# A recommendation tower's pairwise dot products: the second tile's gram of each pair made sample by sample in two banks, packed by one transpose

## The reference

```
e = stack([tbl_f[ids[:, f]] for f in range(32)], axis=1)      # 2048 x 32 x 128
z = einsum('bfd,bgd->bfg', e, e)[:, iu, ju]                   # upper triangle: 496
h = concatenate([z, dense_ctx], axis=1)                       # 512
h = maximum(h @ W_top1 + b_top1, 0);  h = maximum(h @ W_top2 + b_top2, 0)
y = h @ W_top3                                                # 2048 x 1
```

## Time and profile before

| | |
|---|---|
| median of 3 executions | 439.18 us (438.72 to 439.19) |
| the profiled execution | 440.8 us |
| its span, first to last instruction | 438.9 us |
| TensorE matmuls busy | 396.6 us, 90% |
| VectorE busy | 337.4 us, 77% |
| GpSimd busy | 307.6 us, 70% |
| ScalarE busy | 121.7 us, 28% |
| mean granted TensorE clock | 0.984 |

### The profile page before, as it was taken

How to read it: one execution, slowest core, us unless ns; L and a number is a source line. 1 busy time by engine, 2 the same in 40 slices (tenths; PEclk the granted TensorE clock), 3 DMA queues, 4 the chain that set the end, 5 groups by cost and what they waited for, 6 DMA issues and landing times.

```text
span 438.9 us, 11697 instructions
## 1 busy us (share of the span) xinstructions
PE 396.6 (90%) x4672; PEld 371.2 (85%) x4672; DVE 337.4 (77%) x873; ACT 121.7 (28%) x220; POOL 307.6 (70%) x324
## 2 busy tenths in 40 slices
PE   0469677999999999999999999999999999999967
PEld 0468577989999889989999989999999999998866
DVE  3789949999498958899498949899589949891510
ACT  1254410133213321233113321233214311332323
POOL 5777877777777777777777777777777777777100
PEclk9998998899999999999999999999999999999999
DMA  6999953435234332424332442436332543332000
GB/s 131 235 240 215 218 174 80 104 78 100 77 83 77 99 98 57 99 75 103 74 81 72 106 93 58 97 79 100 73 86 72 102 93 66 89 74 54 21 3 2
DMA packets 31374, 42.11 MB, mean 96 GB/s; under 512 B 11164, under 2 KB 24220, under 8 KB 31352
## 3 DMA queue, kind: packets, MB, share of 16 engines
q1 hardware_dynamic: 18936, 20.64, 22.7%
q0 software_dynamic: 10240, 20.99, 18.9%
q10 hardware_dynamic: 2176, 0.17, 0.4%
HBM read 41.77 MB, written 0.01 MB: 95 GB/s over the span
## 4 chain that ended last, share of the span: by engine, by line
PE 55%; DVE 28%; issue 6%; DMA 5%; SPq 3%; ACT 1%; DVEq 0%; ACTq 0%
PE sel_ps L295 19%; DVE onehot L628 17%; PE gram_ps L314 12%; PE work_ps L352 11%; DVE pairs L639 9%; PE work_ps L360 6%; DMA pairs<-tables_selected 5%; PE work_ps L277 3%; PE work_ps L425 2%; SPq L227 1%; SPq L222 1%; DVE table_lo L662 1%; PE work_ps L434 1%; PE work_ps L331 1%; DVE pairs L653 1%
## 5 line engine op out<-in xcount | busy, mean ns | idle before, releaser
L248 POOL DMA_INDIRECT gathered<-table,tile_ids x320 | 307.4, 960 | 100.3 <-issue 95.4
L628 DVE TENSOR_SCALAR onehot<-id_rows,row_no 128x256 fp32r<-128x256 int32 x768 | 238.8, 386 | 19.4 <-DMA id_rows<-ids_selected 12.2
L295 PE MATMUL sel_ps<-onehot,table_hi 125*128 125x256 f32 x768 | 202.0, 300 | 30.1 <-DVE table_lo L662 23.1
L295 PE MATMUL sel_ps<-onehot,table_lo 125*128 125x256 f32 x768 | 194.5, 290 | 0.0
L295 PEld LDWEIGHTS sel_ps<-onehot,table_hi 125*128 125x128 f32 x768 | 152.1, 198 | 38.8 <-DVE table_lo L662 24.0
L295 PEld LDWEIGHTS sel_ps<-onehot,table_lo 125*128 125x128 f32 x768 | 152.7, 199 | 0.0
L639 DVE STREAM_TRANSPOSE pairs<-gram_ps 32x1024 f32<-32x1024 f32 x60 | 74.8, 1246 | 56.0 <-PE gram_ps L314 55.3
L487 ACT ACTIVATE rows_T<-sel_ps 128x512 f32<-128x512 f32 x48 | 30.0, 627 | 127.3 <-PE sel_ps L295 91.9
L314 PEld LDWEIGHTS gram_ps<-rows_T 128*64 128x64 f32 x1920 | 57.5, 138 | 7.2 <-issue 7.2
L478 ACT ACTIVATE rows_T<-work_ps 128x512 f32<-128x512 f32 x80 | 45.5, 599 | 61.1 <-PE work_ps L277 61.1
L314 PE MATMUL gram_ps<-rows_T 128*64 128x64 f32 x1920 | 59.6, 223 | 2.4 <-issue 2.4
(11 more groups left out here) (26 smaller groups left out, 84.1 us busy)
## 6 DMA issues: line engine op xcount, KB each, us to landing
id_rows<-ids_selected SPq DMA_DIRECT2D x48, 256.0 KB
gathered<-table,tile_ids POOLq DMA_INDIRECT x320
pairs<-tables_selected SPq DMA_DIRECT2D x6, 448.0 KB
x<-tables_selected SPq DMA_DIRECT2D x6, 448.0 KB
w_sb<-w SPq DMA_DIRECT2D x1, 1024.0 KB
w_sb<-w SPq DMA_DIRECT2D x1, 512.0 KB
pairs<-tables_selected SPq DMA_DIRECT2D x6, 52.0 KB
x<-tables_selected SPq DMA_DIRECT2D x6, 52.0 KB
```

The costliest lines, as they stand in the source:

```text
L248: nc.gpsimd.indirect_dma_start(gathered[:, t, g, :], None, tables_gathered[g], bass.IndirectOffsetOnAxis(ap=slot_id, axis=0)).then_inc(chu ...
L295: last_op = nc.tensor.matmul(sel_ps[:, u % 2, e, :], part[0:SEL_P, 2 * u + e, k, :], onehot[0:SEL_P, (2 * u + h) % HALF_SLOTS, kk, e, :], ...
L628: last_op = nc.vector.tensor_scalar(onehot[:, (2 * u + h) % HALF_SLOTS, kk, e, :], id_rows[:, slot, e, :], row_no[:, k:k + 1], None, ALU.i ...
```

## The change

The gram of the second tile of every pair is now made as the last tile's was: one sample in a call in the first two banks of `gram_ps`, and one 128x1024 transpose packs it. That is one gram in the prologue and one in each of the six passes of the loop, seven in all; the last tile is as it was. The first tiles keep two samples in a call, in four banks. The helpers are renamed (`gram_doubles`, `turn_doubles`, `turn_singles`), and `singles` no longer depends on the tile.

```
-        def singles(t):
-            return gram_ps[:, t * P * N_FEAT // 4:(t + 1) * P * N_FEAT // 4].rearrange("p (s g) -> p s g", g=N_FEAT)
+        def singles():
+            return gram_ps[:, 0:P * N_FEAT // 4].rearrange("p (s g) -> p s g", g=N_FEAT)
...
             def gram_singles(t):
                 for s in range(P // 4):
                     for j in range(4):
                         rows = rows_T[:, t, 4 * s + j, :]
-                        last_op = nc.tensor.matmul(singles(t)[32 * j:32 * j + 32, s, :], rows, rows,
+                        last_op = nc.tensor.matmul(singles()[32 * j:32 * j + 32, s, :], rows, rows,
                                                    start=True, stop=True)
...
             gram_waits(0, 0, 1)
-            gram_part(1, 0, P // 4).then_inc(gram_done, 1)
+            gram_singles(1)
...
                 gram_waits(i, 1, 1)
-                gram_part(1, 0, 32).then_inc(gram_done, 1)
+                gram_singles(1)
...
-            def turn_gram_singles(i, o, t):
-                dve.wait_ge(gram_done, at(i, o, 2, t + 1))
-                nc.vector.transpose(pairs[:, t, :, :], singles(t).rearrange("p s g -> p g s")
+            def turn_singles(i, o):
+                dve.wait_ge(gram_done, at(i, o, 2, 2))
+                nc.vector.transpose(pairs[:, 1, :, :], singles().rearrange("p s g -> p g s")
                                     ).then_inc(gram_read, 1)
...
             def to_first_gram(i, o):
-                for q in range(4):
-                    turn_gram(i, o - 1, 1, q)
+                turn_singles(i, o - 1)
                 compare(i, o, 3, (1,))
                 merge_pairs(i, o - 1, 1)
```

More of the change, by code:

```diff
@@ L306, in gram_waits, with gram_doubles @@
                     pe.wait_ge(gram_read, at(i, o, 2, t))
-            def gram_part(t, first, n):
-                for s in range(first, first + n):
+            def gram_doubles(t):
+                for s in range(P // 4):
                     for j in range(2):
@@ L315, in gram_part @@
                                                    start=True, stop=True)
-                return last_op
+                last_op.then_inc(gram_done, 1)
             def gram_singles(t):
@@ L385, in to_first_gram @@
                 gram_waits(i, o, 0)
-                gram_part(0, 0, 32).then_inc(gram_done, 1)
+                gram_doubles(0)
                 turn(i, o, 6)
@@ L397, in _ @@
             gram_waits(0, 0, 0)
-            gram_part(0, 0, P // 4).then_inc(gram_done, 1)
+            gram_doubles(0)
             select(0, 1, 0)
@@ L631, in compare, with turn_doubles @@
                     last_op.then_inc(onehot_ready, 1)
-            def turn_gram(i, o, t, q):
+            def turn_doubles(i, o, q):
                 if q == 0:
-                    dve.wait_ge(gram_done, at(i, o, 2, t + 1))
+                    dve.wait_ge(gram_done, at(i, o, 2, 1))
                 quadrant = slice(32 * q, 32 * q + 32)
-                last_op = nc.vector.transpose(pairs[quadrant, t, :, :],
+                last_op = nc.vector.transpose(pairs[quadrant, 0, :, :],
                                               doubles()[quadrant, :, q % 2, :].rearrange("p s g -> p g s"))
@@ L680, in gram0_and_next @@
                 for q in range(4):
-                    turn_gram(i, o, 0, q)
+                    turn_doubles(i, o, q)
                 compare(i, o + 1, 1, (1,))
@@ L706, in _ @@
             for q in range(4):
-                turn_gram(0, last, 0, q)
+                turn_doubles(0, last, q)
             merge_pairs(0, last, 0)
-            turn_gram_singles(0, last, 1)
+            turn_singles(0, last)
             merge_pairs(0, last, 1)
```

## The result

| | before | changed |
|---|---|---|
| median of 20 executions each | 439.28 us (436.56 to 442.71) | 436.55 us (433.56 to 438.82) |
| the profiled execution, its span | 440.8, 438.9 us | 438.4, 436.5 us |

The ratio of the times is 0.9938, with a 95% interval of 0.9909 to 0.9966. The change makes the kernel faster by 2.7 us. The prediction was 432.4 us with a range of 430.9 to 436.0: the sign was right, the size was less than half of it, and the time lies outside the range.

The account below looks back on a forecast made before the run. GpSimd's gathers, 50.0 us a pair, were the bound; TensorE, cut from 48.8 to 45.8, would catch up, gaining only the last chunk's 6.86 us: 440.8 - 6.8 = 434.0 profiled, 1.62 lower in the median, 432.4 (range 430.9 to 436.0).

Parts of the forecast that it names:

- GpSimd's stream as the bound: Whole loop: gathers need 50.0 us a pair; TensorE catches up, so the gain ends at the last chunk's 6.86 us.
- VectorE's 1.4 us a pass: Loop: earlier packing removes TensorE's waits for one-hot matrices in units 3 to 5, together 1.4 us a pair.
- TensorE's 1.6 us a pass: Loop's second gram: single-sample calls take 2.3 us in place of 3.88, a gain of 1.6 us a gram.
- In the loop I take the value without the hole: Loop's new gram: taken at the tail's 2.3 us without its hole, not 4.7 us with it.
- the sum for TensorE alone: Loop: TensorE's pair falls from 48.8 to 45.8 us by the 1.6 and 1.4 us gains.
- Six times: Loop: TensorE's gain of 3.0 us a pair was counted for six pairs, the first pass included.
- The prologue's term: Prologue: a gain of 1 to 3 us after its gram's hole, charged as a loss of 0.8.
- The tail "that the change leaves alone": After the last chunk 9 is turned: last tile's gram and layers stay at 22.4 us.
- that case: Last pair: a clock slowed after TensorE's waits could cost 1 to 1.5 us, putting the end at 434.
- The rival: Loop's single-sample gram has a 2.3 us hole each pass, 4.7 us in all; time 433.6 to 436; chance 0.10.

Follow-up runs that it names:

- e6: Kernel before, with one packing transpose in place of four for the second tiles' grams (half the packed values wrong): 434.31 us beside 438.0, ratio 0.9899.
- e17: Kernel before, with each tile's two-sample gram packed by three transposes in place of four: 433.97 us beside 438.79, ratio 0.9888.
- e5: Changed kernel with four packing transposes in place of one, for all tiles but the last: 444.62 us beside 438.0, ratio 1.0121.
- e3: Changed kernel with the gathers of pairs 1 to 7 left out, reusing pair 0's rows: 448.11 us, run once.
- e7: Changed kernel with the prologue's second gram made and packed as before: 435.16 us beside 438.0, ratio 0.9936.
- e9: Changed kernel with TensorE's loop written out six times: 459.45 us beside 437.79 for the kernel before, run once.
- e10: Kernel before with TensorE's loop written out six times: 439.7 us beside 437.79, run once.
- e8: Changed kernel with the loop's gram woven into layer 2, 16 gram calls after each of its 8 matmuls: 440.66 us beside 438.0, ratio 1.0042.
- e11: Changed kernel with the first tiles' grams also made sample by sample and packed by one transpose: 457.67 us beside 437.79 for the kernel before.

## Why the prediction was wrong

**GpSimd's stream as the bound: right, but the changed kernel did not reach it.** In e6 and e17, TensorE catches up and then goes at the gathers' pace, and chunk 9 is turned at 408.06 and 409.38, where the forecast had 409.7. The changed kernel turned it at 412.12, 1.8 us after the gathers' last packet, since what was to bring it there was too small. These 2.4 us and 2.0 in the tail are the whole miss of the profiled execution, 438.4 in place of 434.0.

**VectorE's 1.4 us a pass: right.** e6 gives 1.4 by itself, e5, which lacks it, loses more than that again, and e17 shows that 1.2 us of the 3.8 are enough, as waits of 0.3 to 0.5 us had suggested.

**TensorE's 1.6 us a pass: the step that failed.** "In the loop I take the value without the hole" carried the tail's rate over to the loop. It measured 3.66 us, so 0.2 us less than before in place of 1.6, and layer 3 and chunk 0 behind it took 1.25 to 1.6 us in place of 0.9, so TensorE's net gain was nothing. The tail's gram ran after GpSimd had ended; in the loop each gather stops TensorE's issue twice. Shown by e3: 2.20 us without gathers, and a pass of 45.55 where the sum for TensorE alone had 45.8. I had looked only for instruction packets, of which q8 indeed has none to speak of (the earlier trace rows also hold two of q14, which I passed over; the changed kernel has them at the same times and one more, and no hole of a gram falls there), and not for what else differs between the tail and the loop. Weighing the stretch in which a row was measured would have found it. 1.4 us over five later passes is 7 us on TensorE.

**"Six times": the first pass is fresh code too.** I charged a hole to the prologue and none to the first pass, whose instruction packets I had quoted. It measured 4.15 us in the changed kernel and 3.21 in e7; e9 and e10, and the packets beside the very first gram, show the cause. The prologue's term (1 to 3 us gained) came out at about nothing by e7, whose interval leaves room for 1 us and hardly for 3.

**The tail "that the change leaves alone"** took 24.3 us in place of 22.4 in the profiled execution: 0.3 by its hole and 1.6 by the clock after it. The prediction kept that case for the last pair's waits, not for the hole. It was at full clock before, with the same hole of 2.3 us. This goes either way, with the old gram as with the new: of the ten traces of undisturbed runs, the kernel before, e6, e7 and e8 end 22.2 to 22.5 us after chunk 9, and the changed kernel, e5, e9, e10, e11 and e17 end 23.7 to 24.3 after it, with the granted clock at 0.50 for a part of the first layer. The hole's length doesn't decide it: with 2.62 us from start to start e8 kept its clock, and with 2.12 e9 lost it.

The terms of the two profiled executions, by the starts of TensorE's instructions in the two traces: 3.4 us gained when the first pass's second gram starts (2.6 of them because the kernel before had a hole of 2.38 us in its very first gram, which is no effect of the change), 4.3 lost by that gram, 0.7 lost from there to the next pass's first gram, where the slow clock took more than the packing gave, and 6.0 gained over the next five passes, which is 4.4 at the last chunk 9; less 2.0 in the tail it is 2.4 us. That this is near the 2.7 us of the medians is in part luck: the first gram's hole and the tail's clock are accidents of the two executions, one for each side.

**The rival** with sustained issue slower in the loop was the nearest in kind. It held 4.7 us for a gram of each pass, and left out the first pass as well.

Against the rule of the Trainium skill, TensorE: Matmul & The Clock Gate, on the back-to-back gap (25 ns from start to start at least), e3 sustains 256 records in 2.20 us, 8.6 ns each, where the prediction's row gave 9.3 or less; the measurement decides here. Against the capacity that the Trainium skill, Runtime: NRT & Kernel Launch, section on instruction fetch mechanics, gives, 2048 instructions, stands e11: a body of some 1640 weight loads and matmuls is fetched again in every second pass, while the changed kernel's 1380 are kept but for one packet at 233 us and the tail's first at 386.

## What to carry to other kernels

Before a rate is carried from one stretch of a trace to another, list what every other engine does in the two stretches; here GpSimd, whose gathers are for a later gram, set the price. Count instructions as a cost of their own: small calls in code that runs once can wait for their fetch, and so can the first pass of a loop. Where an engine is late by half a microsecond, look for the cheapest half microsecond: one packing instruction less in four, on both tiles, did what the whole change was for.

## What was not expected of the hardware

- A gather of 0.94 us on GpSimd stops TensorE's issue twice, for some 0.28 us each from start to start of the weight loads around it. The two-sample gram, 30 ns a matmul, hides it (3.88 us with gathers and without), that of 8.6 ns doesn't. Gathers slow VectorE too: 32 comparisons take 9.82 us with them and 8.59 without.
- Holes of 1.5 to 4.4 us in a run of small calls in fresh code, and at times in the two-sample calls of the very first gram. They are some of the difference between executions.
- In the disturbed runs the same program takes 43 to 46% longer. For stretches of some 8 to 16 us during or just after GpSimd's gathers TensorE issues one instruction in 1.4 us or so; e3, whose gathers end with pair 0, took 448.11 us there. Why was not found out.
